# Attention and gated feed-forward over 8192 tokens: copies and normalisations of the first four groups on ScalarE or VectorE by expected time, scores in pairs of units, normalisations queued later

## The reference

```python
xn = _layernorm(x)                                   # over the last axis, no scale or shift
latent = xn @ Wc_down                                # 1024 -> 512
q = (latent @ Wq_up).reshape(B, T, 16, 64)
k, v = split(latent @ Wkv_up)                        # one head of 64 for all 16 query heads
att = softmax(causal(q . k / sqrt(64)))
s = (att @ v).reshape(B, T, 1024) @ Wc_proj
h = _silu(xn @ wg.T) * (xn @ wu.T)                   # hidden 3072; int32 weights times 1/127
g = _silu(h @ wd.T)
out = x + s * g
```

## Time and profile before

| | us |
|---|---|
| median of 3 runs (1540.68, 1543.37, 1683.09) | 1543.4 |
| the profiled execution | 1539.7 |
| its span, slowest core | 1538.2 |
| TensorE busy | 1416.0 |
| ScalarE busy | 1197.9 |
| VectorE busy | 634.7 |
| GpSimd busy | 340.1 |

### The profile page before, as it was taken

One profiled execution on the slowest core, in us unless ns is written; L12 is line 12 of the kernel. 1 busy time (PEld: TensorE's weight loads), 2 busy tenths in 40 slices (PEclk: granted clock), 3 DMA queues, 4 the chain that ended last, 5 costly groups with the idle time before them and its releaser, 6 DMA issues.

```text
span 1538.2 us, 44936 instructions; the slowest of 8 cores (1525.6 to 1538.2 us)
## 1 busy us (share of the span) xinstructions
PE 1416.0 (92%) x18064; PEld 791.6 (51%) x18064; DVE 634.7 (41%) x1165; ACT 1197.9 (78%) x1254; POOL 340.1 (22%) x480
## 2 busy tenths in 40 slices
PE   2787999889899999999999999999999999999995
PEld 2554555555555554555555455555555555544442
DVE  4586666673636244251332333312233222134323
ACT  3555878778798989989999899899999999941110
POOL 3553433322121312142121100102130000111003
PEclk9898999989999999999999999999999999999998
DMA  9731423445454727366031122133132222345434
GB/s 237 147 112 56 105 79 95 105 112 117 119 117 117 160 65 189 106 132 159 33 114 63 50 70 71 38 116 111 50 118 70 70 64 83 112 145 195 156 121 157
DMA packets 67386, 166.78 MB, mean 108 GB/s; under 512 B 8048, under 2 KB 17520, under 8 KB 67184
## 3 DMA queue, kind: packets, MB, share of 16 engines
q1 hardware_dynamic: 54576, 132.31, 27.6%
q0 software_dynamic: 12608, 31.59, 11.4%
HBM read 152.47 MB, written 34.60 MB: 122 GB/s over the span
## 4 chain that ended last, share of the span: by engine, by line
PE 78%; issue 5%; DVE 5%; ACT 4%; DMA 4%; POOL 2%; SPq 0%; DVEq 0%; POOLq 0%; ACTq 0%
PE ps L226 77%; ACT p_sb L940 3%; DMA xt<-xb 3%; PE ps L237 2%; DMA wgu_sb<-wgub 1%; DVE bnd L566 1%; DVE g_sb L703 0%; DMA wdr<-wdb 0%; POOL acc_sb L859 0%; DVE h_sb L718 0%; DVE acc_sb L767 0%; DVE xn L409 0%; ACT xn L405 0%; POOL p_sb L947 0%; SPq L250 0%
## 5 line engine op out<-in xcount | busy, mean ns | idle before, releaser
L940 ACT ACTIVATE p_sb<-ps,nbias 128x1024 bf16<-128x1024 f32 x1024 | 1059.0, 1123 | 100.5 <-PE ps L226 83.4
L226 PE MATMUL ps<-vaug,p_sb 128*128 128x65 bf16 x8192 | 383.9, 194 | 21.5 <-DVE y_sb L990 14.2
L226 PEld LDWEIGHTS ps<-vaug,p_sb 128*128 128x128 bf16 x8192 | 306.5, 97 | 179.1 <-issue 147.6
L226 PE MATMUL ps<-own_f,wgu_sb 128*128 128x512 bf16 x1536 | 383.4, 382 | 10.7 <-DVE g_sb L703 3.4
L226 PE MATMUL ps<-qT,kT 64*128 64x256 bf16 (+1 forms) x4352 | 367.6, 271 | 14.4 <-DVE xnT L469 4.8
L226 PEld LDWEIGHTS ps<-qT,kT 64*128 64x128 bf16 x4352 | 150.6, 94 | 234.7 <-issue 204.1
L947 POOL TENSOR_TENSOR p_sb<-p_sb,mask_sb 128x512 bf16<-128x512 bf16 x64 | 74.2, 1160 | 622.0 <-ACT p_sb L940 621.9
L226 PEld LDWEIGHTS ps<-own_f,wgu_sb 128*128 128x128 bf16 x1536 | 131.2, 98 | 136.8 <-issue 24.2
L226 PE MATMUL ps<-wdr,h_sb 128*128 128x512 bf16 x768 | 192.8, 381 | 9.2 <-DMA wdr<-wdb 2.5
L703 DVE COPY g_sb<-ps 128x512 f32<-128x512 f32 x72 | 49.7, 691 | 173.5 <-PE ps L226 173.3
L226 PEld LDWEIGHTS ps<-wdr,h_sb 128*128 128x128 bf16 x768 | 64.6, 98 | 70.9 <-issue 17.5
(11 more groups left out here) (97 smaller groups left out, 1046.8 us busy)
## 6 DMA issues: line engine op xcount, KB each, us to landing
wgu_sb<-wgub SPq DMA_DIRECT2D x72, 512.0 KB, 3.3
xt<-xb SPq DMA_DIRECT2D x57, 512.0 KB, 5.4
wdr<-wdb SPq DMA_DIRECT2D x72, 256.0 KB, 5.3
wgu_sb<-wgu POOLq DMA_DIRECT2D x24, 512.0 KB, 6.9
wgub<-wgu_sb SPq DMA_DIRECT2D x24, 512.0 KB, 6.7
xo_t<-xo SPq DMA_DIRECT2D x32, 256.0 KB, 3.9
out<-acc_sb POOLq DMA_DIRECT2D x32, 256.0 KB, 4.4
wdr<-wd POOLq DMA_DIRECT2D x24, 256.0 KB, 7.7
```

What stands on the lines that cost most here:

```text
L226: return p.op("tensor", lambda e: e.matmul(out, lhsT, rhs, start=start, stop=stop, skip_group_check=shared), waits, "pe" if tok else None, ...
L940: ex = A(cost, lambda en, dst=dst, src=src, bias=bias: en.activation(dst, src, AF.Exp, bias=bias, scale=0.125), [mm, p_prior(u)[1], bias_t ...
```

## The change

Six edits. The planner expects lower transfer rates while a queue is within its first 45 us. A helper `either` compares when ScalarE and VectorE would be done, and gives an operation to the one that is expected first; it is used for the wc copies, the xnT copies and the normalisations of the first four groups, and the small copies of each teff half go all to one engine. A normalisation is written only when its rstd (or nmr) is expected to be there. The main loop sends scores in pairs also with two buffers, and a lone unit only where it is the last of its query block. Values, projection transposes and the closing step get conditions of order.

```diff
     RATE = {"sync": 250.0, "gpsimd": 170.0}
+    FIRST = {"sync": 165.0, "gpsimd": 107.0}
...
-            self.dma_t[engine] = max(self.dma_t[engine], t) + dma / self.RATE[engine]
+            at = max(self.dma_t[engine], t)
+            self.dma_t[engine] = at + dma / (self.RATE if at > 45e3 else self.FIRST)[engine]
...
+        def either(ca, emit_a, cv, emit_v, waits=()):
+
+            w = ready(*[t for t in waits if t is not None])
+            ta = max(p.T["scalar"], w) + ca + p.LAT["scalar"]
+            tv = max(p.T["vector"], w) + cv + p.LAT["vector"]
+            return A(ca, emit_a, waits) if ta < tv else V(cv, emit_v, waits)
...
-                if q % 2:
-                    ev = V(690, lambda e, dst4=dst4, src4=src4: e.tensor_copy(dst4, src4), [mm])
-                else:
-                    ev = A(930, lambda e, dst4=dst4, src4=src4: e.activation(dst4, src4, AF.Copy), [mm])
+                ev = either(930, lambda e, dst4=dst4, src4=src4: e.activation(dst4, src4, AF.Copy),
+                            690, lambda e, dst4=dst4, src4=src4: e.tensor_copy(dst4, src4), [mm])
...
+                on_a = p.T["scalar"] < p.T["vector"]
...
-                yield lambda j=j: 0.0 if j < 4 or j - 4 in tp_done else INF
+                yield lambda j=j, a=a: ready(a) if j < 4 or j - 4 in tp_done else INF
...
                 if shared:
-                    w = A(1150, lambda e, j=j, xs=xs: e.activation(
+                    w = either(1150, lambda e, j=j, xs=xs: e.activation(
                         xn[:, j % 4, :], xs, AF.Identity, bias=nmr[:, j % 8:j % 8 + 1],
-                        scale=rstd[:, j % 8:j % 8 + 1]), [a, xn_free[j % 4]])
+                        scale=rstd[:, j % 8:j % 8 + 1]), 830, on_v, [a, xn_free[j % 4]])
...
                 if g < PRO:
-                    ev = A(930, lambda e, dst8=dst8, src8=src8: e.activation(dst8, src8, AF.Copy),
-                           [mm] + xnT_free[0])
+                    ev = either(930, lambda e, dst8=dst8, src8=src8: e.activation(dst8, src8, AF.Copy),
+                                690, lambda e, dst8=dst8, src8=src8: e.tensor_copy(dst8, src8),
+                                [mm] + xnT_free[0])
...
-                if (e, nh) not in fetched and (e, nh) in s_spill:
-                    yield lambda: INF if held[r] else 0.0
-                    fetch(e, nh)
+            yield lambda: 0.0
+
+            if (e, nh) not in fetched and (e, nh) in s_spill:
+                yield lambda: INF if held[r] else 0.0
+                fetch(e, nh)
             direct = (e, nh) in fetched
-            yield lambda: 0.0
...
+            if last and e > 0 and (e - 1, hg // 2) not in epi_done:
+                return INF
...
-            yield lambda: max(ready(yt), bank_t())
+            yield lambda: max(ready(yt), bank_t(), 0.0 if e < 2 or e - 2 in proj_done else INF)
...
-                    if n >= (2 if nbuf == 3 else 1) and tn > t0:
+                    if n >= 2 and tn > t0:
                         break
                     at = max(at, tn)
                     n += 1
-                if n:
+                if n >= 2 or n and (nu + n == NU or units[nu + n][0] > units[nu][0]):
                     offer(at, ("s", n))
```

More of the change, by code:

```diff
@@ L351, in gen_teff @@
                 ms = slice(4 * hf, 4 * hf + 4)
+                evs = []
+                on_a = p.T["scalar"] < p.T["vector"]
                 for out, col in ((teffk[:, ms, 0:64], 0), (teffk[:, ms, 64:128], 0), (teffv[:, ms, :], 64)):
                     src = tf_v[:, :, col:col + 64]
[L354 to L359, removed]
+                    evs.append(A(350, lambda e, out=out, src=src: e.activation(out, src, AF.Copy), [mm]) if on_a else
+                               V(350, lambda e, out=out, src=src: e.tensor_copy(out, src), [mm]))
+                give(b, evs)
+                teff_tok.extend(evs)
             h_free.append(mm)
@@ L402, in ln_tiles @@
                 xs = x_tile(j)
-                yield lambda j=j: 0.0 if j < 4 or j - 4 in tp_done else INF
+                yield lambda j=j, a=a: ready(a) if j < 4 or j - 4 in tp_done else INF
+                on_v = lambda e, j=j, xs=xs: e.tensor_scalar(
+                    xn[:, j % 4, :], xs, mv[:, j % 8, 0:1], rstd[:, j % 8:j % 8 + 1], ALU.subtract, ALU.mult)
                 if shared:
-                    w = A(1150, lambda e, j=j, xs=xs: e.activation(
+                    w = either(1150, lambda e, j=j, xs=xs: e.activation(
                         xn[:, j % 4, :], xs, AF.Identity, bias=nmr[:, j % 8:j % 8 + 1],
-                        scale=rstd[:, j % 8:j % 8 + 1]), [a, xn_free[j % 4]])
+                        scale=rstd[:, j % 8:j % 8 + 1]), 830, on_v, [a, xn_free[j % 4]])
                 else:
-                    w = V(830, lambda e, j=j, xs=xs: e.tensor_scalar(
-                        xn[:, j % 4, :], xs, mv[:, j % 8, 0:1], rstd[:, j % 8:j % 8 + 1],
-                        ALU.subtract, ALU.mult), [a, xn_free[j % 4]])
+                    w = V(830, on_v, [a, xn_free[j % 4]])
                 q = x_place(j)
@@ L484, in gen_group @@
             xnT_tok[g] = evs
-            yield lambda: max(ready(*teff_tok, *evs) if len(teff_tok) == 2 else INF, bank_t())
+            yield lambda: max(ready(*teff_tok, *evs) if len(teff_tok) == 6 else INF, bank_t())
             b, fr = take()
@@ L1005, in gen_epi @@
             y_free[r] = mm
+            epi_done.add((e, r))
             ev = V(430, lambda en: en.tensor_copy(yT[:, par, 4 * r:4 * r + 4, :],
@@ L1014, in build_program @@
         s_free = [None, None]
+        proj_done = set()
+        epi_done = set()
         def gen_proj(e):
@@ L1046, in gen_proj @@
             yT_free[par] = mm
+            proj_done.add(e)
         class Work:
```

## The result

The changed kernel takes 1523.4 us (median; 1522.5 to 1528.5), the kernel before 1542.0: 0.989 of it, 95% interval 0.986 to 0.992. It is faster by some 19 us where I had forecast 60, and outside my range of 1458 to 1520. The interval is clear of 1, but the gain is under the 2% (1512.5) from which the prediction called a kernel faster. Its profiled execution has a span of 1521.2 us on the slowest core.

The account below looks back on a forecast made before the run. TensorE's total work was taken as the bound. From 1539.7 us: pairs -44, their waits +8, later normalisations -14, free engines at the start -10, giving 1479.7; plus 3.7 to the median, 1483 us. Range for 8 in 10: 1458 to 1520.

Parts of the forecast that it names:

- The switches: TensorE's score matmuls: 436 lone units merge into 218 pairs, each saving 0.20 us, 44 us in all.
- Only idle time that takes its place can eat this: TensorE, scores in pairs: a switch costs the same wherever it lies, so only new idle time can reduce the 44 us.
- The 8 us: TensorE's price for waiting on the second score buffer: 218 x 1.11 us at 2% to 7% idle, 5 to 17 us.
- Rival (a): TensorE finds no filler for a fifth of the pairs' waits (48 us); pair rule worth nothing, 1523 us; chance 0.14.
- The slip of the attention: New ScalarE gaps delay the attention by 60 us, to end near 1398, costing nothing because feed-forward is left.
- The row for a gap: ScalarE's gap per pair, from first score matmul to exponential: 0.55 to 0.98 us, 120 to 214 us for 218 pairs.
- rival (b): ScalarE becomes the bound, each pair costing it 0.98 us: 1561 us; decides from a slip of about 132 us; chance 0.06.
- The late normalisations: VectorE no longer stalls on rstd from GpSimd, mostly from 130 to 340: 14 us gained, bounds 0 and 21.
- The start: First four groups, copies and normalisations on either engine, with new transfer rates: 10 us gained, bounds 0 and 32.
- hidden: Eight of 16 normalisations moved to VectorE cost it 6 us more, covered by its idle time from 40 to 130.
- rival (c): Planner's clock wrong about GpSimd and arrivals; later normalisations and free copies bring nothing: 1507 us; chance 0.20.
- VectorE against GpSimd: Shared port pair: if the engines block each other, GpSimd loses up to 6 us; first part gains 4, not 10.

Follow-up runs that it names:

- pairs alone: The kernel before with only the pair rule and the guards; transfer rates, engines and normalisations as before: 1.0027 of the kernel before.
- pairs_late_two: Changed kernel with old transfer rates, pairs only from query block 9 on, no third score buffer in blocks 9 and 10: 0.982 of the kernel before.
- two_buffers: Changed kernel with old transfer rates and never a third score buffer: 1643.8 us, 1.0685 of the kernel before.
- Late pairs: Changed kernel with old transfer rates, old lone-unit rule in query blocks 0 to 8, pairs from block 9 on: 1512.7 us, 0.983 of the kernel before.
- three orders of the changed kernel: Changed kernel as it was and with one planner latency nudged by 6 ns (ScalarE's, then TensorE's): 0.9891, 0.9911, 0.9917 of the kernel before.
- no_late_norm: Changed kernel with normalisations written as soon as VectorE's expected time allows, as before: 1542.2 us, 0.9997 of the kernel before.
- late_from_5: Changed kernel with old transfer rates and late normalisations only from the fifth group on: 0.997 of the kernel before.
- three orders without pairs: Changed kernel with the old lone-unit rule, as it was and with ScalarE's or TensorE's planner latency nudged by 6 ns: 0.9885, 0.9896, 0.9895 of the kernel before.
- all pairs with old rates: Changed kernel without the lower transfer rates of the first 45 us, pairs everywhere: 1518.0 us, 0.984 of the kernel before.

## Why the prediction was wrong

**The switches were right.** The cost of 0.20 and, nearly, the count: in the trace 732 uninterrupted runs of score matmuls became 531, 201 x 0.20 = 40 us, against 44. In the written order all 436 lone units went, as forecast, but some of them had stood next to other scores, with no switch between.

**"Only idle time that takes its place can eat this": it did, and I priced it at 8.** This is the step that failed. Here is TensorE's time before and with pairs alone (the slowest core of each; both traces have all 18064 matmuls). It is worked out from the starts of all matmuls: each is given its steady distance to the next (29 ns for values, 54.5 for scores, 56 and 216 for the 128 and 512 wide), and what a distance has above that is a switch, a wait when it is over 250 ns, or the rest:

| us | before | pairs alone |
|---|---|---|
| steady work | 1198.9 | 1198.9 |
| switches | 141.8 | 101.5 |
| waits | 118.8 | 148.9 |
| rest | 48.0 | 67.9 |
| before the first and after the last matmul | 31 | 28 |

Switches gave 40 and waits took 30 of it. The rest took 20: what matmuls that start at the lower clock level lose against their steady distance goes from 17 to 32 us, so 15 of the 20 are the clock, and 5 are delays too short to count as waits. These are slowest cores; over the six cores of each run whose traces are complete, the median of all waits together goes from 117 to 143 us and the median loss at the lower level from 14.5 to 24. Busy time by stretch, before and with pairs alone, each from 130 on:

```profile
130.00:400.00 270.00, 245.65 (x3667) 148.70 (x3665) 164.61 (x327) 217.08 (x222) 91.09 (x146) 0.96 0.37 96
400.00:700.00 300.00, 284.05 (x3954) 161.33 (x3952) 127.41 (x240) 266.06 (x276) 75.50 (x109) 0.99 0.55 132
...
130.00:400.00 270.00, 236.33 (x3144) 145.49 (x3143) 176.25 (x339) 178.65 (x186) 86.49 (x146) 0.94 0.48 128
400.00:700.00 300.00, 278.10 (x3730) 159.96 (x3730) 125.61 (x230) 246.77 (x257) 80.62 (x111) 0.97 0.52 138
```

TensorE is idle 9 and 6 us more, and the granted clock goes from 0.96 and 0.99 to 0.94 and 0.97; while TensorE had work, its clock was at the lower of the two levels (1.2 GHz) for 55 us in all before and for 99 with pairs (the medians of the six cores are 46 and 72). I had counted the clock as a gain of the late normalisations and not as a price of the pairs' waits.

The 8 us were the wait for the second buffer alone, at the idle share of the kernel before. That wait stayed small (8.8 us for exponentials, 10.8 with pairs alone). What I did not price is what the filler needs: a bank, and an engine to empty it. The written order has the third score buffer out for some 820 of 1088 units with pairs, for some 640 without, and then one bank is left for feed-forward, groups and projections. And early, the filler that replaces scores brings 14 us more of copies and products to VectorE, in whose queue TensorE's other results stand. Two of TensorE's sums of waits that grew with pairs alone are these; before they were 6.7 us for h_sb and 1.4 for p_sb, which GpSimd masks:

```profile
PE ps L228 <- DVE h_sb L725: 11.3, 19, 3.0
PE ps L228 <- POOL p_sb L955: 7.5, 6, 1.9
```

So part of the 30 us is a wait for GpSimd's masks, which neither I nor a rival named; that the banks and VectorE's queue make the rest is argued from these rows and from pairs_late_two, and not shown. Rival (a) had this effect (the rule worth nothing, a chance of 0.14) and named the one bank that is left. But its sign, tens of us of waits for exponentials, did not come, and that its 1523 is what was measured is luck: it holds 10 us for the start that never came.

**The slip of the attention was mis-sized by two.** I took 60 us and an end near 1400. The last exponential starts at 1483.8, against 1360.5: 123 us later, and some 140 with what the late normalisations and the engines took out. The row for a gap was nearly right (0.55 to 0.98; measured 1.09 over 161 waits), but the idle time that ScalarE had already did not absorb it. This is past my own point of decision of rival (b), 132 us, which was worked out for an end near 1470; with the end at 1521 there are still 17 us of feed-forward behind the last exponential. So the pairs did not make ScalarE the bound here, but they used up nearly all the slack; two_buffers shows the far side. Late pairs leave 102 us of filler, and it is there that they gain.

**The late normalisations were right, in mechanism and size.** 14 forecast, 13 measured alone and 16 in the changed kernel, with the waits gone that were named. What came with them was named too, at nothing: the x loads go later, and VectorE waits 31.8 us for x where it had 19.1 (33.7 in the changed kernel). It is paid within the 13.

**The start brought nothing.** I took 10 us. TensorE was to wait less for copies, and the waits for h_sb and xnT did fall, but xn took their place. In order of time, ScalarE and VectorE at group 1:

```profile
47.21 2.37 ACT L414 ACTIVATE xn<-wdr,nmr,rstd 128x1024 bf16<-128x1024 f32 x2 [10.05 <-POOL nmr L407]
47.23 1.54 DVE L411 TENSOR_SCALAR xn<-wdr,mv,rstd 128x1024 bf16<-128x1024 f32 x2 [2.37 <-POOL nmr L407]
```

Against 32.99 in the earlier trace rows. The step that failed is the word "hidden" for the work that goes to VectorE: I asked whether VectorE had time for it, and not what would stand behind it in VectorE's queue. In the changed kernel the second half of tile 7's statistics is written behind a copy that waits for TensorE:

```profile
32.00 0.67 DVE L384 BATCH_NORM_STATS2 st<-wdr 128x6 f32<-128x512 f32 x1
40.85 0.69 DVE L498 CAST kT<-ps 128x512 bf16<-128x512 f32 x1 [8.18 <-PE ps L228]
41.46 0.68 DVE L387 BATCH_NORM_STATS2 st<-wdr 128x6 f32<-128x512 f32 x1
```

The late rule, which holds the next tiles' statistics together with the normalisation, has a part in it, but neither it nor the free engines do it alone. rstd of group 1 comes at 32 to 33 in the two kernels with old engines and without the late rule, at 35 in the two with old engines and the rule, and at 44 to 50 in all fourteen with free engines and the rule (in three orders of the changed kernel 46, 44 and 44). With free engines and no late rule it came at 36 once (no_late_norm) and at 46 once (late_from_5). What the loss at the start is worth in time is small: the changed kernel is at 0.989 to 0.992 in its three orders, and 0.987 without free engines, so they bring nothing or cost up to 5 us. Without the late rule they also put 24 us of waits for nmr on VectorE. So one half of rival (c) came true, that the free copies bring nothing, and the other half, that the later normalisations bring nothing, did not.

**VectorE against GpSimd.** The rows showed 1.5 us for a normalisation beside GpSimd, which at 102.87 was not only masking, as I wrote, but also squaring and copying own tokens. At 47.23 two take 1.54, 0.77 each, with GpSimd issuing a transfer only. The Trainium skill (SBUF — State Buffer, "Who interferes with whom") has the two engines block each other on the shared pair; neither row contradicts it, but the start's loss of the changed kernel lies in the order above, and no run here was made to price the lock.

**The sum anew**, from 1542 for the kernel before: pairs 0 to +2 (low rates), late normalisations -13, rates and engines -3 (0.991 with the late rule alone, 0.989 as the mean of three orders without pairs, a difference inside the intervals): 1526 to 1528, with an order's scatter of 4. The changed kernel and its two nudges lie at 1523, 1527 and 1528. This adds up measured parts and is no test of them.

What stays open: how the pairs' 30 us of waits divide between banks, VectorE's order and GpSimd's masks, and why all pairs with old rates are not slower than late ones by what the early ones lose. The spared banks took 5 us of idle time away in one stretch; the rest was not parted. The guards, which the prediction took at nothing, are in every kernel but the one before, and no run parts them from the rest.

## What to carry to other kernels

Work taken off the fullest engine counts only if what fills its place needs nothing scarce: before pricing it, name the buffer and the copying engine that the filler will ask for, and add the lower clock that each new wait may bring. Batch the switches where there is slack on the second engine, and stay with single steps where there is none; here the same rule lost 7 us in the first nine blocks and won 8 in the last seven, the first tried in one order and the second in two. And where a program's order is written by a planner, nudge it by a number that means nothing before believing a difference of a few us: here such a nudge moved the time by up to 4.

## What the runs showed of the hardware

TensorE's clock fell more often where the kernel had more short waits, without longer ones: with pairs alone the longest wait after 130 us is 4.0 us (6.5 before), waits of over 250 ns are 180 instead of 138, and the time at the lower level while TensorE had work rose from 55 to 99 us, 17 of the 44 before 130 us and 27 after. The two go together here; that one causes the other was not tried by itself. In two_buffers, where TensorE after 1300 works in bursts between exponentials (busy 266 of 342 us), the granted clock of that stretch is 0.84.

In every trace the clock records hold the two levels 1.0 and 0.5 alone.
